# A three-pass f32 matmul kernel on one core: the work of its first tiles in another order

## The chip, the cores and the metric

The kernel runs on one core of a Trainium2 chip. The metric is the device time of one execution in microseconds, as the median of several; lower is better. The engines are TensorE (PE, with its weight loads PEld), VectorE (DVE), ScalarE (ACT), GpSimd (POOL) and SyncE (SP). Each runs its own instructions in the order of the program and waits on semaphores. SP issues most DMAs here, POOL some of them.

## The reference, cut to what matters

Eight images x of 512 tokens by 2048 features go through two adapters of rank 16, chosen per image, and a dense layer.

```
# layer 0: a low-rank update of x, adapters chosen by ids0
Bx  = einsum('bni,bri->bnr', x, B[ids0]);  x = x + einsum('bnr,bor->bno', Bx, A[ids0])
# layer 1: dense layer, bias and a second low-rank update, adapters chosen by ids1
base = einsum('bti,oi->bto', x, W) + b
lora = einsum('bti,bir->btr', x, lora_A[ids1]);  lora = einsum('btr,bro->bto', lora, lora_B[ids1])
out  = x + base + lora * 2
```

## The kernel before, in words

**The big product.** Two images make a group; there are four groups. In a group the product of x1 (x after layer 0) with W plus the identity is computed from halves of W and of x by seven products of sums of halves instead of eight. A product i has 8 output tiles o, so a group has 56 steps and the kernel 224; step s is (g, i, o). A step takes 8 blocks c of 128 input rows. Each operand is split into a high and a low part (w_hi, w_lo, x_hi, x_lo), and a block takes three matmuls of 128x512: L695, L696, L697. Such a step is 24 matmuls.

**Weights.** load_w(s) on SP loads w_one, and w_two where the product needs a sum of two blocks of W; that is so in group 0 for products 0, 1, 2, 4 and 6. make_w(s) on DVE adds the two (L887) and the identity (L891), keep_sum(s) on SP stores the sum in w_sums (L445), and later groups load it from there. Then split_w(s): ACT makes w_hi (L740), DVE w_lo (L896). There are three w_one buffers and two of each other, and load_w(s + 3) is issued in step s, behind keep_sum(s + 1).

**The two adapters' first halves.** "Down": x of an image is multiplied with the adapters of both layers, in 8 chunk pairs d per image. ACT and DVE split each pair (split_chunk(d), L780 and L927), PE runs four matmuls into down_ps (project_down, L640 and L641). Image 1 comes first, as pairs 0 to 7, then image 0. copy_down, add_down and split_rank_x make rank_x from it. "Up": project_up(v) multiplies rank_x with up_w, two matmuls into up_ps (L653), and add_up(v) on DVE adds them to x (L946). v counts the quarters of half an image; B1, A0, B0 and A1 name the four halves of a group, a being the group's first image and b its second. Then sum_x(p, r) and split_x(p, r) (L910, L913; L758, L919) make x_hi and x_lo of product p, quarter r. x_hi and x_lo have six buffers; buffers 4 and 5 lie where a1_raw and a0_raw were.

**The images.** After step 4, 16 matmuls multiply the tables of a0 and a1 (L724), and four more (make_image, L661) fold them into the rank-16 rows that add_rank uses. Their results are copied out by DVE (L1064).

**What sets the order.** It is written by hand: a prologue in each engine's block, and tables by step: ups(s), downs(s), load_at, sum_at and split_at. In a step DVE goes through add(s - 1), split_w(s + 1), split_x, sum_x, add_down, split_down, make_w(s + 2), split_chunk, split_rank_x, split_up, add_up, complete and the copy of an image.

Of the kernel before, what the change touches and what calls it, by code (L numbers as in the profile page):

```python
# [12 lines left out]
NB = 8  # L13
# [40 lines left out]
def load_at(p):  # L54

    return (1, 2, 5, 6) if p % PRODUCTS == 2 else (0, 1, 3, 5)


def sum_at(p):

    if p == 1:
        return (5, 5, 6, 7)
    return {1: (2, 3, 5, 6), 2: (2, 3, 6, 7)}.get(p % PRODUCTS, (1, 3, 5, 6))


def split_at(p):

    if p == 1:
        return (6, 6)
    return {0: (3, 5), 1: (4, 5), 2: (4, 5)}.get(p % PRODUCTS, (2, 4))  # L70
# [37 lines left out]
def ups(s):  # L108

    if s >= STEPS:  # L110
        return []
    if s < 0:
        return [0, 1]
    g, i, o = where(s)
    found = [2, 3] if s == 0 else []
    if i == 0:
        found += [16 * g + 4 * A0 + r for r, at in enumerate((1, 2, 4, 5) if g else (4, 4, 5, 5)) if at == o]
    found += [16 * g + 4 * B0 + r for r, at in enumerate((7, 8, 10, 11)) if at == s % PER_GROUP]
    if i == 2:
        found += [16 * g + 4 * A1 + r for r, at in enumerate((1, 3, 5, 7)) if at == o]  # L120
    if i == 6 and g + 1 < GROUPS:
        found += [16 * (g + 1) + r for r, at in enumerate((2, 4, 5, 6)) if at == o]
    return found
# [134 lines left out]
def build(nc, x, ids0, ids1, a0_down, a0_up, b0, w, bias, a1, b1, identity, mask, w_sums, images, x1, out):  # L258
    with ExitStack() as ctx:
# [99 lines left out]
        down_added = sem("down_added")  # L359
        rank_x_hi_ready = sem("rank_x_hi_ready")  # L360
        rank_x_ready = sem("rank_x_ready")
        rank_loaded = sem("rank_loaded")
# [38 lines left out]
        def down_parts(e):  # L401

            if e < 8:
                return x_hi[e // 2][:, e % 2, :], x_lo[e // 2][:, e % 2, :]
            return bg_hi[e % 3][:, :], bg_lo[e % 3][:, :]

        def rank_x_of(n):
# [12 lines left out]
        def _(sp):  # L420
# [88 lines left out]
            sp.dma_start(ids_sb[:, 1, :], ids1).then_inc(ids_loaded, DMA)  # L509
            for d in (0, 1):  # L510
                load_raw("down", d)
            for d in (2, 3):
                load_early(d)
            sp.wait_ge(ids_loaded, 2 * DMA)
            sp.dma_start(down_raw[0][:, :, :], adapter(0, 1, b0).rearrange("u p c r -> (u p) c r")).then_inc(first_down_loaded, DMA)
            sp.dma_start(down_raw[1][:, :, :], adapter(1, 1, a1).rearrange("u p c r -> (u p) c r")).then_inc(first_down_loaded, DMA)
            for r in range(CH):
                load_resident(0, 1, r)
# [11 lines left out]
            for s in range(STEPS):  # L530
# [8 lines left out]
                if s + W_ONES < STEPS:  # L539
                    load_w(s + W_ONES)  # L540
                if s in (1, 2):
                    for n in range(4 * s - 4, 4 * s):
                        sp.dma_start(a1_raw[:, n, :, :], adapter(1, n, a1).rearrange("u p c r -> (u p) c r"))\
                          .then_inc(a1_loaded, DMA)
# [22 lines left out]
        def _(pool):  # L567
# [38 lines left out]
            load_up(0)  # L606
            load_down(0)
            for n in range(NB):
                pool.dma_start(a0_raw[:, n, :, :], adapter(0, n, a0_down).rearrange("u p c r -> (u p) c r"))\
                    .then_inc(a0_loaded, DMA)  # L610
# [17 lines left out]
        def _(pe):  # L628
            def project_down(d):
                n, k = down_chunk(d)  # L630
                if k == 0:
                    pe.wait_ge(down_ready, turn(n) + 1)
                    if turn(n):
                        pe.wait_ge(down_added, turn(n))
                for u in range(2):
                    pe.wait_ge(bg_ready, 2 * d + u + 1)
                    c = 2 * k + u
                    hi, lo = down_parts(2 * d + u)
                    weights = down[:, c, :, :, :].rearrange("p h l r -> p (h l r)")
                    pe.matmul(down_ps[:, :], weights, hi, start=(c == 0), stop=False)  # L640
                    pe.matmul(down_ps[:, :], weights, lo, start=False, stop=(c == C - 1)).then_inc(bg_used, 1)  # L641

            def project_up(v):
                n, half, r = up_chunk(v)
                if r == 0:
                    pe.wait_ge(up_ready, v // 4 + 1)
                    pe.wait_ge(rank_x_ready, turn(n) + 1)
                for u in range(2):
                    e = 2 * v + u
                    if e >= 2:  # L650
                        pe.wait_ge(up_added, e - 1)
                    o = 2 * r + u
                    pe.matmul(up_ps[e % 2][:, :], up_w[:, P * o:P * (o + 1)], rank_x_of(n)[:, :], start=True, stop=True)\  # L653
                      .then_inc(up_done, 1)

            def make_image(j):
                pe.wait_ge(across_ready, 1)
                pe.wait_ge(b1_rows_loaded, NB * DMA)
                if j:
                    pe.wait_ge(image_ready, j)  # L660
                pe.matmul(image_ps[:, :], across, rows[:, T * j:T * (j + 1)], start=True, stop=True).then_inc(image_done, 1)  # L661

            def add_rank(s):
# [4 lines left out]
                if o == 0:  # L668
                    pe.wait_ge(rank_ready, rank_number(g, i) + 1)
                    pe.wait_ge(rank_x_ready, turn(2 * g + side) + 1)  # L670
                if i == 4:
                    pe.wait_ge(copied, copied_before(s) + 1)
# [58 lines left out]
        def _(act):  # L731
# [42 lines left out]
            def split_chunk(d):  # L774

                wait_for_down_source(act, d)
                for e in (2 * d, 2 * d + 1):
                    if e >= 11:
                        act.wait_ge(bg_used, e - 2)
# [12 lines left out]
            def split_down(n):  # L792
# [4 lines left out]
                if turn(n):  # L797
                    act.wait_ge(down_added, turn(n))
                act.activation(down[:, :, 0, 0, :], down_raw[0][:, :, :], ACT.Copy)
                act.activation(down[:, :, 0, 1, :], down_raw[1][:, :, :], ACT.Copy, scale=SCALE1).then_inc(down_hi_ready, 1)  # L800

            def copy_down(n):
                act.wait_ge(bg_used, 16 * (turn(n) + 1))
                if turn(n):
                    act.wait_ge(rank_x_ready, turn(n))
                act.activation(rank_sum[:, :], down_ps[2 * R:4 * R, :], ACT.Copy).then_inc(down_copied, 1)

            def split_rank_x(n):
# [5 lines left out]
                x_rank = rank_x_of(n)  # L814
                act.activation(x_rank[0:2 * R, :], rank_sum[:, :], ACT.Copy)
                act.activation(x_rank[2 * R:4 * R, :], rank_sum[:, :], ACT.Copy).then_inc(rank_x_hi_ready, 1)

# [11 lines left out]
            split_chunk(3)  # L829
            split_chunk(4)  # L830
            split_up(0)
            split_w(0)
            for d in (5, 6, 7):
                split_chunk(d)
            copy_down(1)
            split_rank_x(1)
            for r in range(CH):
                split_x(0, r)
            split_down(0)
            for d in downs(0):  # L840
                split_chunk(d)
            for s in range(STEPS):
# [6 lines left out]
                if s >= 1 and where(s - 1)[1] == 1:  # L849
                    copy(s - 1)  # L850
                if s == 3:
                    act.wait_ge(a1_loaded, NB * DMA)
                    act.activation(a1_cols.rearrange("p (c n r) -> p c n r", c=C, n=NB),
                                   a1_raw[:, :, :, :].rearrange("p n c r -> p c n r"), ACT.Copy).then_inc(a1_ready, 1)
                if p + 1 < PRODUCTS * GROUPS:
# [9 lines left out]
                if s and s in RANK_X_AT:  # L865
                    split_rank_x(RANK_X_AT[s])
                if s in UP_SPLIT:
                    split_up(UP_SPLIT[s])
# [7 lines left out]
        def _(dve):  # L876
# [131 lines left out]
            split_chunk(2)  # L1008
            split_chunk(3)
            make_w(0)  # L1010
            split_chunk(4)
            split_up(0)
            split_w(0)
            for d in (5, 6, 7):
                split_chunk(d)
            make_w(1)
            add_down(1)
            split_rank_x(1)
            for v in range(CH):
                add_up(v)  # L1020
                split_x(0, v)
            split_down(0)
            for d in downs(0):
                split_chunk(d)
            for s in range(STEPS):
# [4 lines left out]
                if s >= 1:  # L1030
                    add(s - 1)
                if s < STEPS - 1:
                    split_w(s + 1)
                if p + 1 < PRODUCTS * GROUPS:
                    for r in range(2):
# [14 lines left out]
                if s in UP_SPLIT:  # L1050
                    split_up(UP_SPLIT[s])
                if s:
                    for v in ups(s):
                        add_up(v)
                if s >= 1:
# [5 lines left out]
                if 0 <= s - 1 - IMAGE_STEP < 4:  # L1061
                    j = s - 1 - IMAGE_STEP
                    dve.wait_ge(image_done, j + 1)
                    dve.tensor_copy(rows[:, T * j:T * (j + 1)], image_ps[:, :]).then_inc(image_ready, 1)  # L1064
                if (i, o) in RANK_SPLIT:
# [42 lines left out]
```

## Time and profile before

| | us |
|---|---|
| median of 3 runs | 1412.16 (1412.0 to 1413.15) |
| the profiled execution | 1413.14 |
| its span | 1411.1 |
| PE busy | 1368.4 (97%) |
| DVE busy | 951.0 (67%) |
| ACT busy | 552.6 (39%) |
| POOL busy | 86.4 (6%) |
| mean DMA rate | 229 GB/s |

The span runs from the first to the last recorded instruction. Busy times of engines overlap, so they don't add up; an idle engine costs something only where another waits for it. The granted clock of TensorE is 1.00 (2.4 GHz) but for some stretches before 90 us, where it is down to 0.50 (1.2 GHz).

### The profile page before, as it was taken

How to read it: one execution, taken by the hardware profiler on the slowest of the kernel's cores; microseconds unless marked ns; L12 is line 12 of the kernel's file. 1: busy time of each engine (PE TensorE's matmuls, PEld its weight loads, DVE VectorE, ACT ScalarE, POOL GpSimd, SP SyncE). 2: the span in 40 equal slices, each digit the busy share in tenths (PEclk: the TensorE clock that was granted, in tenths of full speed). 3: DMA queues.
4: the chain of work that ended last, by engine and by line, in shares of the span. 5: the costliest groups of instructions: out<-in, count | busy, mean ns of one | idle time of the engine just before them, and what ended most of it. 6: DMA issues, size and time to landing. Idle time of an engine off the chain costs nothing.

```text
span 1411.1 us, 16438 instructions
## 1 busy us (share of the span) xinstructions
PE 1368.4 (97%) x5928; PEld 1116.9 (79%) x5928; DVE 951.0 (67%) x1143; ACT 552.6 (39%) x666; POOL 86.4 (6%) x179
## 2 busy tenths in 40 slices
PE   3888999999999999999999999999999999999999
PEld 2676777888888888888888888888888888888887
DVE  5768876888875666667855676666875566655662
ACT  4443423446334432345523442344633443223321
POOL 2000001000000001010000000110010000000000
PEclk8899999999999999999999999999999999999999
DMA  9768995999973666577853556575973366545542
GB/s 351 217 228 300 356 368 193 324 361 345 329 260 128 220 223 205 182 258 241 290 181 123 183 193 241 167 246 204 326 240 125 124 225 227 192 157 196 197 150 82
DMA packets 101332, 323.15 MB, mean 229 GB/s; under 512 B 13508, under 2 KB 15044, under 8 KB 100996
## 3 DMA queue, kind: packets, MB, share of 16 engines
q1 hardware_dynamic: 95188, 307.68, 62.7%
q0 software_dynamic: 6064, 14.43, 3.6%
q8 instruction: 47, 0.77, 0.2%
q14 instruction: 33, 0.27, 0.1%
HBM read 249.70 MB, written 72.35 MB: 228 GB/s over the span
## 4 chain that ended last, share of the span: by engine, by line
PE 87%; DVE 4%; DMA 4%; ACT 2%; issue 1%; SPq 1%; DVEq 0%; ACTq 0%
PE acc L695 26%; PE acc L696 26%; PE acc L697 26%; DMA w_two<-w 4%; PE acc L675 2%; PE down_ps L640 2%; PE down_ps L641 2%; PE up_ps L653 2%; DVE w_one L887 1%; DVE bg_raw L946 1%; ACT w_hi L740 1%; DVE resident L946 1%; DVE x_lo L919 0%; DMA bg_raw<-x 0%; ACT x_hi L758 0%
## 5 line engine op out<-in xcount | busy, mean ns | idle before, releaser
L695 PE MATMUL acc<-x_hi,w_hi 128*128 128x512 f32 x1792 | 703.0, 392 | 6.6 <-DVE x_lo L919 3.7
L696 PE MATMUL acc<-x_lo,w_hi 128*128 128x512 f32 x1792 | 700.5, 391 | 0.0
L697 PE MATMUL acc<-x_hi,w_lo 128*128 128x512 f32 x1792 | 700.2, 391 | 0.0
L740 ACT ACTIVATE w_hi<-w_one 128x1024 fp32r<-128x1024 f32 x224 | 237.0, 1058 | 544.5 <-PE acc L697 491.1
L896 DVE TENSOR_TENSOR w_lo<-w_one,w_hi 128x1024 fp32r<-128x1024 f32 x224 | 274.2, 1224 | 227.7 <-ACT w_hi L740 227.0
L695 PEld LDWEIGHTS acc<-x_hi,w_hi 128*128 128x128 f32 x1792 | 337.9, 189 | 82.8 <-issue 6.9
L696 PEld LDWEIGHTS acc<-x_lo,w_hi 128*128 128x128 f32 x1792 | 338.0, 189 | 73.1 <-issue 1.0
L697 PEld LDWEIGHTS acc<-x_hi,w_lo 128*128 128x128 f32 x1792 | 337.4, 188 | 71.6
L772 ACT ACTIVATE sums<-acc 128x512 f32<-128x512 f32 x96 | 56.9, 593 | 192.3 <-PE acc L697 186.5
L979 DVE SCALAR_TENSOR_TENSOR sums<-acc,bias_sb,sums 128x512 f32<-128x512 f32 x128 | 95.5, 746 | 25.5 <-PE acc L675 25.1
L919 DVE TENSOR_TENSOR x_lo<-x_stage,x_hi 128x1024 fp32r<-128x1024 f32 x80 | 96.0, 1219 | 2.9 <-ACT x_hi L758 2.7
L758 ACT ACTIVATE x_hi<-x_stage 128x1024 fp32r<-128x1024 f32 x80 | 83.9, 1051 | 13.7 <-PE acc L697 8.1
L913 DVE TENSOR_TENSOR x_stage<-x_stage,resident 128x1024 f32<-128x1024 f32 x64 | 77.9, 1217 | 0.0
L780 ACT ACTIVATE bg_hi<-bg_raw 128x512 fp32r<-128x512 f32 x100 | 58.5, 622 | 38.0 <-DMA bg_raw<-x 34.9
L927 DVE TENSOR_TENSOR bg_lo<-bg_raw,bg_hi 128x512 fp32r<-128x512 f32 x100 | 64.4, 684 | 5.4 <-ACT bg_hi L780 5.4
L589 POOL DMA_DIRECT2D rank_raw<-images x48 | 23.4, 487 | 650.1 <-issue 649.8
L887 DVE TENSOR_TENSOR w_one<-w_one,w_two 128x1024 f32<-128x1024 f32 x40 | 48.8, 1219 | 17.0 <-DMA w_two<-w 17.0
L640 PE MATMUL down_ps<-bg_hi,down 128*128 128x512 f32 x120 | 50.1, 418 | 7.9 <-DVE bg_lo L927 7.9
L603 POOL DMA_DIRECT2D rank_raw<-a_up x48 | 23.5, 491 | 516.5 <-issue 515.9
L966 DVE TENSOR_TENSOR sums<-sums,acc 128x512 f32<-128x512 f32 x32 | 22.0, 686 | 47.7 <-PE acc L697 47.6
L653 PE MATMUL up_ps<-rank_x,up_w 96*128 96x512 f32 x128 | 43.2, 417 | 9.1 <-DVE rank_x L995 3.5
L675 PE MATMUL acc<-rank_x,rank_w 96*128 96x512 f32 x128 | 50.9, 398 | 0.0
(60 smaller groups left out, 668.7 us busy)
## 6 DMA issues: line engine op xcount, KB each, us to landing
w_one<-w_sums SPq DMA_DIRECT2D x120, 512.0 KB, 4.3
w_one<-w SPq DMA_DIRECT2D x104, 512.0 KB, 5.5
bg_raw<-x SPq DMA_DIRECT2D x84, 512.0 KB, 6.1
x_stage<-x SPq DMA_DIRECT2D x68, 512.0 KB, 5.1
out<-sums SPq DMA_DIRECT2D x128, 256.0 KB, 3.6
w_two<-w SPq DMA_DIRECT2D x40, 512.0 KB, 8.1
w_sums<-w_one SPq DMA_DIRECT2D x40, 512.0 KB, 5.6
resident<-x SPq DMA_DIRECT2D x32, 512.0 KB, 8.1
```

What stands on the lines that cost most here:

```text
L640: pe.matmul(down_ps[:, :], weights, hi, start=(c == 0), stop=False)
L653: pe.matmul(up_ps[e % 2][:, :], up_w[:, P * o:P * (o + 1)], rank_x_of(n)[:, :], start=True, stop=True)\
L675: pe.matmul(acc[s % BANKS][:, :], rank_w[:, P * o:P * (o + 1)], rank_x_of(2 * g + side)[:, :], start=False, stop=True, skip_group_check=Tr ...
L695: pe.matmul(ps[:, :], w_hi[ws][:, c, :], hi, start=(c == 0), stop=False)
L696: pe.matmul(ps[:, :], w_hi[ws][:, c, :], lo, start=False, stop=False)
L697: mm = pe.matmul(ps[:, :], w_lo[ws][:, c, :], hi, start=False, stop=(c == H - 1))
L740: act.activation(w_hi[s % W_PARTS][:, :, :], w_one[s % W_ONES][:, :, :], ACT.Copy).then_inc(w_hi_ready, 1)
L758: act.activation(x_hi[q % X_PARTS][:, :, :], x_source(p, r), ACT.Copy).then_inc(x_hi_ready, 1)
L896: dve.tensor_tensor(w_lo[s % W_PARTS][:, :, :], w_one[s % W_ONES][:, :, :], f32(w_hi[s % W_PARTS][:, :, :]), ALU.subtract).then_inc(w_read ...
L913: dve.tensor_tensor(stage, stage, resident[1 if i in (3, 6) else 0][:, cs, :], ALU.subtract if i in (2, 6) else ALU.add).then_inc(x_summed, 1)
L919: dve.tensor_tensor(x_lo[q % X_PARTS][:, :, :], x_source(p, r), f32(x_hi[q % X_PARTS][:, :, :]), ALU.subtract).then_inc(x_ready, 1)
L979: dve.scalar_tensor_tensor(out=tile, in0=acc[s % BANKS][:, :], scalar=bias_sb[:, f:f + 1], in1=tile, op0=ALU.add, op1=ALU.add).then_inc(ba ...
```

## The change

On SP the loads of the first adapters move ahead of the x loads of pairs 1, 2 and 3. In the prologue of ACT and DVE the up weights are split before pair 4, pairs 4 to 7 come before make_w(0) and split_w(0), and split_w(0), split_down(0) and the first pair of image 0 come before the first add_up; add_up(1) comes before split_x(0, 0), and make_w(1) stands behind the last split_x. Pairs 4 and 5 use x_hi and x_lo buffers, and so POOL and SP hold the tables of a0 and a1 until 12 halves of pairs are used. rank_x has a semaphore of its own for ACT's second half. The copy of a1 on ACT comes after split_rank_x in step 3. The up pairs of A0 in group 0 go to steps 4, 5, 6 and 6 (they were in 4, 4, 5 and 5), those of B0 to 8, 9, 11 and 12 in all groups (7, 8, 10 and 11). In each step the first add_up moves ahead of split_w, a second one right behind it. Images alternate between two banks.

```diff
 def load_at(p):
-    return (1, 2, 5, 6) if p % PRODUCTS == 2 else (0, 1, 3, 5)
+    return (2, 3, 5, 6) if p % PRODUCTS == 2 else (0, 1, 3, 5)
...
     if p == 1:
-        return (5, 5, 6, 7)
-    return {1: (2, 3, 5, 6), 2: (2, 3, 6, 7)}.get(p % PRODUCTS, (1, 3, 5, 6))
+        return (4, 5, 6, 7)
+    return {1: (2, 3, 5, 6), 2: (3, 4, 6, 7)}.get(p % PRODUCTS, (1, 3, 5, 6))
...
     if p == 1:
-        return (6, 6)
+        return (5, 6)
...
-        found += [16 * g + 4 * A0 + r for r, at in enumerate((1, 2, 4, 5) if g else (4, 4, 5, 5)) if at == o]
-    found += [16 * g + 4 * B0 + r for r, at in enumerate((7, 8, 10, 11)) if at == s % PER_GROUP]
+        found += [16 * g + 4 * A0 + r for r, at in enumerate((1, 2, 4, 5) if g else (4, 5, 6, 6)) if at == o]
+    found += [16 * g + 4 * B0 + r for r, at in enumerate((8, 9, 11, 12)) if at == s % PER_GROUP]
...
-            if e < 8:
+            if e < 12:
                 return x_hi[e // 2][:, e % 2, :], x_lo[e // 2][:, e % 2, :]
...
+        def image_bank(j):
+            return down_ps if j % 2 else image_ps
...
-            for d in (0, 1):
-                load_raw("down", d)
-            for d in (2, 3):
-                load_early(d)
+            load_raw("down", 0)
             sp.wait_ge(ids_loaded, 2 * DMA)
...
+            load_raw("down", 1)
+            for d in (2, 3):
+                load_early(d)
...
+                if s == 1:
+                    sp.wait_ge(bg_used, 12)
...
+            pool.wait_ge(bg_used, 12)
             for n in range(NB):
...
+                    if turn(n) == 2:
+                        pe.wait_ge(image_ready, 4)
...
                     pe.wait_ge(rank_x_ready, turn(n) + 1)
+                    pe.wait_ge(rank_x_copied, turn(n) + 1)
...
-                if j:
-                    pe.wait_ge(image_ready, j)
+                if j >= 2:
+                    pe.wait_ge(image_ready, j - 1)
...
                 if turn(n):
-                    act.wait_ge(down_added, turn(n))
+                    act.wait_ge(bg_used, 16 * turn(n))
...
-                act.activation(x_rank[0:2 * R, :], rank_sum[:, :], ACT.Copy)
-                act.activation(x_rank[2 * R:4 * R, :], rank_sum[:, :], ACT.Copy).then_inc(rank_x_hi_ready, 1)
+                act.activation(x_rank[0:2 * R, :], rank_sum[:, :], ACT.Copy).then_inc(rank_x_hi_ready, 1)
+                act.activation(x_rank[2 * R:4 * R, :], rank_sum[:, :], ACT.Copy).then_inc(rank_x_copied, 1)
```

The prologue on DVE; ACT's has the same order. First before, from the split of pairs 2 and 3 (x_lo from x_stage) to the first add_up (L946):

```order
L927 TENSOR_TENSOR x_lo<-x_stage,x_hi 128x512 x4
L887 TENSOR_TENSOR w_one<-w_one,w_two 128x1024
L891 SCALAR_TENSOR_TENSOR w_one<-identity_sb,w_one 128x128
L927 TENSOR_TENSOR bg_lo<-resident,bg_hi 128x512 x2
L932 TENSOR_TENSOR up_w<-rank_raw,up_w 16x1024
L896 TENSOR_TENSOR w_lo<-w_one,w_hi 128x1024
L927 TENSOR_TENSOR bg_lo<-resident,bg_hi 128x512 x6
...
L991 TENSOR_TENSOR rank_sum<-down_ps,rank_sum 32x512
L995 TENSOR_TENSOR rank_x<-rank_sum,rank_x 32x512
L946 TENSOR_TENSOR resident<-resident,up_ps 128x512 x2
L919 TENSOR_TENSOR x_lo<-resident,x_hi 128x1024
```

And the same place of the changed kernel, whose line numbers are 12 higher here:

```order
L939 TENSOR_TENSOR x_lo<-x_stage,x_hi 128x512 x4
L944 TENSOR_TENSOR up_w<-rank_raw,up_w 16x1024
L939 TENSOR_TENSOR x_lo<-resident,x_hi 128x512 x4
L939 TENSOR_TENSOR bg_lo<-resident,bg_hi 128x512 x4
L899 TENSOR_TENSOR w_one<-w_one,w_two 128x1024
...
L1003 TENSOR_TENSOR rank_sum<-down_ps,rank_sum 32x512
L1007 TENSOR_TENSOR rank_x<-rank_sum,rank_x 32x512
L908 TENSOR_TENSOR w_lo<-w_one,w_hi 128x1024
...
L939 TENSOR_TENSOR bg_lo<-resident,bg_hi 128x512 x2
L958 TENSOR_TENSOR resident<-resident,up_ps 128x512 x4
L931 TENSOR_TENSOR x_lo<-resident,x_hi 128x1024
```

The sum of the weights (make_w(0)) moved behind all pairs of image 1, w_lo(0) behind rank_x, and split_down(0) with a pair of image 0 moved from behind the last x_lo to ahead of the first add_up; two add_up now stand in a row.

DVE in steps 4 and 5, before:

```order
L946 TENSOR_TENSOR resident<-resident,up_ps 128x512 x4
L896 TENSOR_TENSOR w_lo<-w_one,w_hi 128x1024
L910 TENSOR_TENSOR x_stage<-resident 128x1024 x2
L887 TENSOR_TENSOR w_one<-w_one,w_two 128x1024
L891 SCALAR_TENSOR_TENSOR w_one<-identity_sb,w_one 128x128
L946 TENSOR_TENSOR resident<-resident,up_ps 128x512 x4
L1060 TENSOR_TENSOR sums<-down_ps,sums 128x128
```

And in steps 4 to 6 of the changed kernel:

```order
L958 TENSOR_TENSOR resident<-resident,up_ps 128x512 x2
L908 TENSOR_TENSOR w_lo<-w_one,w_hi 128x1024
L922 TENSOR_TENSOR x_stage<-resident 128x1024
L899 TENSOR_TENSOR w_one<-w_one,w_two 128x1024
L903 SCALAR_TENSOR_TENSOR w_one<-identity_sb,w_one 128x128
L958 TENSOR_TENSOR resident<-resident,up_ps 128x512 x2
L908 TENSOR_TENSOR w_lo<-w_one,w_hi 128x1024
...
L1079 TENSOR_TENSOR sums<-down_ps,sums 128x128
L958 TENSOR_TENSOR resident<-resident,up_ps 128x512 x2
L908 TENSOR_TENSOR w_lo<-w_one,w_hi 128x1024
L958 TENSOR_TENSOR resident<-resident,up_ps 128x512 x2
```

The four adds in a row came apart, and each first one stands ahead of the w_lo of its step.

## Rows read from the trace of the kernel before

**Rows 1.** The page, busy us by engine, share and instructions.
```profile
PE 1368.4 (97%) x5928; PEld 1116.9 (79%) x5928; DVE 951.0 (67%) x1143; ACT 552.6 (39%) x666; POOL 86.4 (6%) x179
```

**Rows 2.** Waits of PE, whole run: us in total, times, longest us.
```profile
PE image_ps L661 <- DVE sums L1064: 2.6, 2, 1.6
PE acc L695 <- DVE w_lo L896: 2.4, 2, 1.3
...
PE up_ps L653 <- DVE up_w L932: 1.3, 1, 1.3
```

**Rows 3.** Timeline of PE: start us, us, engine, line, operation [idle before <-releaser].
```profile
13.22 0.79 PE L640 MATMUL down_ps<-x_hi,down 128*128 128x512 f32 x1 [13.22 <-DVE down L985]
...
35.09 1.14 PE L653 MATMUL up_ps<-rank_x,up_w 96*128 96x512 f32 x2 [3.50 <-DVE rank_x L995]
...
39.69 0.77 PE L695 MATMUL acc<-x_hi,w_hi 128*128 128x512 f32 x1 [1.65 <-DVE x_lo L919]
...
42.39 1.06 PE L653 MATMUL up_ps<-rank_x,up_w 96*128 96x512 f32 x2
...
56.66 0.39 PE L695 MATMUL acc<-x_hi,w_hi 128*128 128x512 f32 x1
...
79.06 0.39 PE L695 MATMUL acc<-x_hi,w_hi 128*128 128x512 f32 x1
...
82.01 0.70 PE L653 MATMUL up_ps<-rank_x,up_w 96*128 96x512 f32 x2 [1.43 <-issue]
...
85.98 1.39 PE L653 MATMUL up_ps<-rank_x,up_w 96*128 96x512 f32 x2 [1.89 <-DVE resident L946]
...
91.12 3.73 PE L724 MATMUL down_ps<-a_raw,sums 128*128 128x128 f32 x32
94.61 0.48 PE L695 MATMUL acc<-x_hi,w_hi 128*128 128x512 f32 x1
...
117.07 1.10 PE L661 MATMUL image_ps<-sums 128*128 128x512 f32 x2 [1.58 <-DVE sums L1064]
...
211.59 0.47 PE L695 MATMUL acc<-x_hi,w_hi 128*128 128x512 f32 x1 [1.30 <-DVE w_lo L896]
```

**Rows 4.** Timeline of DVE, and its waits for w_two after 150 us.
```profile
20.03 1.22 DVE L887 TENSOR_TENSOR w_one<-w_one,w_two 128x1024 f32<-128x1024 f32 x1 [4.45 <-DMA w_two<-w]
...
25.20 1.89 DVE L927 TENSOR_TENSOR bg_lo<-resident,bg_hi 128x512 fp32r<-128x512 f32 x3
...
DVE w_one L887 <- DMA w_two<-w: 12.6, 12, 1.7
```

**Rows 5.** Timeline of ACT.
```profile
11.65 0.42 ACT L799 ACTIVATE down<-down_raw 128x256 fp32r<-128x256 f32 x1 [3.94 <-DMA down_raw<-a]
...
15.40 2.10 ACT L789 ACTIVATE up_w<-rank_raw 16x1024 fp32r<-16x1024 f32 x2
...
76.50 1.91 ACT L853 ACTIVATE sums<-a_raw 128x2048 f32<-128x2048 f32 x1
```

**Rows 6.** DMA issues of SP; 128 KB loads to landing; the bg_raw tile before 60 us.
```profile
5.49 0.35 SPq L516 DMA_DIRECT2D down_raw<-a  x1
...
31.75 0.33 SPq L445 DMA_DIRECT2D w_sums<-w_one  x1
...
110.06 0.33 SPq L445 DMA_DIRECT2D w_sums<-w_one  x1
...
a_raw<-a SPq DMA_DIRECT2D x8, 128.0 KB, 3.2
...
DMA to landing us min/median/max: 3.7/11.4/18.9
```

**Rows 7.** Busy us by engine in a stretch, then PEclk, DMA share, GB/s.
```profile
105.00:110.00 5.00, 5.00 (x21) 3.45 (x19) 4.97 (x6) 4.46 (x5) 0.00 (x0) 1.00 0.01 5
110.00:115.00 5.00, 3.70 (x17) 3.05 (x17) 4.90 (x6) 3.08 (x3) 1.46 (x3) 1.00 0.80 223
...
190.00:200.00 10.00, 8.92 (x40) 7.09 (x39) 7.85 (x9) 2.01 (x2) 0.00 (x0) 1.00 1.00 382
```

More of the change, by code:

```diff
@@ L360, in build @@
         rank_x_hi_ready = sem("rank_x_hi_ready")
+        rank_x_copied = sem("rank_x_copied")
         rank_x_ready = sem("rank_x_ready")
@@ L658, in make_image @@
                 pe.wait_ge(b1_rows_loaded, NB * DMA)
-                if j:
-                    pe.wait_ge(image_ready, j)
-                pe.matmul(image_ps[:, :], across, rows[:, T * j:T * (j + 1)], start=True, stop=True).then_inc(image_done, 1)
+                if j >= 2:
+                    pe.wait_ge(image_ready, j - 1)
+                pe.matmul(image_bank(j)[:, :], across, rows[:, T * j:T * (j + 1)], start=True, stop=True).then_inc(image_done, 1)
             def add_rank(s):
@@ L670, in add_rank @@
                     pe.wait_ge(rank_x_ready, turn(2 * g + side) + 1)
+                    pe.wait_ge(rank_x_copied, turn(2 * g + side) + 1)
                 if i == 4:
@@ L777, in split_chunk @@
                 for e in (2 * d, 2 * d + 1):
-                    if e >= 11:
+                    if e >= 15:
                         act.wait_ge(bg_used, e - 2)
@@ L805, in copy_down @@
                     act.wait_ge(rank_x_ready, turn(n))
+                    act.wait_ge(rank_x_copied, turn(n))
                 act.activation(rank_sum[:, :], down_ps[2 * R:4 * R, :], ACT.Copy).then_inc(down_copied, 1)
@@ L829, in _ @@
             split_chunk(3)
-            split_chunk(4)
             split_up(0)
-            split_w(0)
-            for d in (5, 6, 7):
+            for d in (4, 5, 6, 7):
                 split_chunk(d)
@@ L836, in _ @@
             split_rank_x(1)
+            split_w(0)
+            split_down(0)
+            first, second = downs(0)
+            split_chunk(first)
             for r in range(CH):
                 split_x(0, r)
-            split_down(0)
-            for d in downs(0):
-                split_chunk(d)
+            split_chunk(second)
             for s in range(STEPS):
@@ L850, in _ @@
                     copy(s - 1)
[L851 to L854, printed above, removed]
                 if p + 1 < PRODUCTS * GROUPS:
@@ L866, in _ @@
                     split_rank_x(RANK_X_AT[s])
+                if s == 3:
+                    act.wait_ge(a1_loaded, NB * DMA)
+                    act.activation(a1_cols.rearrange("p (c n r) -> p c n r", c=C, n=NB),
+                                   a1_raw[:, :, :, :].rearrange("p n c r -> p c n r"), ACT.Copy).then_inc(a1_ready, 1)
                 if s in UP_SPLIT:
@@ L1009, in _ @@
             split_chunk(3)
+            split_up(0)
+            for d in (4, 5, 6, 7):
+                split_chunk(d)
             make_w(0)
[L1011 to L1016, printed above, removed]
             add_down(1)
             split_rank_x(1)
-            for v in range(CH):
-                add_up(v)
-                split_x(0, v)
+            split_w(0)
             split_down(0)
-            for d in downs(0):
-                split_chunk(d)
+            first, second = downs(0)
+            split_chunk(first)
+            add_up(0)
+            add_up(1)
+            split_x(0, 0)
+            add_up(2)
+            split_x(0, 1)
+            add_up(3)
+            split_x(0, 2)
+            split_x(0, 3)
+            make_w(1)
+            split_chunk(second)
             for s in range(STEPS):
@@ L1031, in _ @@
                     add(s - 1)
+                us = ups(s) if s else []
+                for v in us[:1]:
+                    add_up(v)
                 if s < STEPS - 1:
                     split_w(s + 1)
+                for v in us[1:]:
+                    add_up(v)
                 if p + 1 < PRODUCTS * GROUPS:
@@ L1051, in _ @@
                     split_up(UP_SPLIT[s])
-                if s:
-                    for v in ups(s):
-                        add_up(v)
                 if s >= 1:
@@ L1063, in _ @@
                     dve.wait_ge(image_done, j + 1)
-                    dve.tensor_copy(rows[:, T * j:T * (j + 1)], image_ps[:, :]).then_inc(image_ready, 1)
+                    dve.tensor_copy(rows[:, T * j:T * (j + 1)], image_bank(j)[:, :]).then_inc(image_ready, 1)
                 if (i, o) in RANK_SPLIT:
```

## The prediction, made before the changed kernel ran

> **What bounds the kernel now.** The totals first [rows 1]: TensorE (PE) is busy 1368.4 of 1411.1 us. Only the other 42.7 us, and matmuls run at half clock, can be won. The list of PE's waits [rows 2] and the timeline [rows 3] put all of them before some 220 us; after the wait at 211.59 one of half a us is left. So the question is how much earlier PE gets past step 23. What follows moves with it.
>
> Four stretches matter. PE starts at 13.22, because ScalarE (ACT) waits until 11.65 for the adapters [rows 3, 5]. The down projection of image 1 (8 chunk pairs, d 0 to 7, four matmuls each) is fed in pieces: after half of it VectorE (DVE) sits 4.45 us waiting for the weights w_two, in front of work that PE wants [rows 4], and the first up projection starts at 35.09. Step 1 starts at 56.66. Steps 4 to 8 have holes: 1.43 and 1.89 us in step 4, 1.3 in step 7 for up_w, 2.6 for two images [rows 2, 3]. Then the DMA engines are full (share 1.00, 382 GB/s, still at 190 to 200 [rows 7]) and DVE waits 12 times for w_two, 12.6 us in all, after 150 us [rows 4]; 2.4 us of that reach PE as waits for w_lo [rows 2].
>
> **Part 1: the adapters ahead of three x loads on SP.** They need the ids and are issued at 4.36 and 5.49 in either order; before, 2 MB of x stood ahead, now 0.5 MB. They were there at 11.65 [rows 5, 6]. Bounds: no gain, or landing at 8.7 (5.49 + 3.2, the median of the later 128 KB loads on that queue [rows 6]). I take 9, and nothing hangs on it: chunk pair 1 is now issued at 5.9, and as the fastest 512 KB load took 3.7 us [rows 6] and the adapters share the way, it lands near 9.9. ACT: 1.1 for pair 1, 0.7 for the adapters; DVE 0.8 behind it; PE starts at 12.7, **0.5 us earlier**. The x of pairs 4 to 7 follows at 1.3 us each (512 KB at 390 GB/s) until 17.4; ACT wants the first at 17.1, the last at 20.3.
>
> **Part 2: pairs 4 to 7 before the weight work.** ACT: pairs 2 and 3 until 14.0, up_w 3.17 (two in 2.10, and a third [rows 5]) until 17.1, then 8 halves at 0.54 until 21.4. DVE: up_w 1.2 until 18.4, then 8 halves at 0.61 (three take 1.89 [rows 4]) until 23.3. PE ends the last near 24.1; before it was 31.4. Then ACT copies 0.6, DVE adds 0.7 (behind make_w(0), 1.5 us, of which the copy hides all but the last), rank_x takes 1.3 + 0.7 + gaps, and the first up projection starts at 27.4: **7.7 us earlier** [rows 3].
>
> **Part 3: step 0, where most of that is paid back.** Ahead of the first add_up DVE now has split_w(0) 1.2 with 1 us of waiting for w_hi(0), split_down(0) 0.7 and a chunk pair 1.2: add_up(0) starts at 31.4. With add_up(1) it is 34.2, with x_lo(0,0) 35.4. The new wait: add_up(2) needs a projection that PE issues only after the first six matmuls of step 0, and these need x_lo(0,0). Six took 2.7 us at half clock (39.69 to 42.39 [rows 3]), which I keep, as PE has just stood idle. So 2.7 + 0.8 until DVE sees the projection + 1.3 + 1.2 go round before x_lo(0,1) is out at 41.3; the same round brings add_up(3) to 44.7; x_lo(0,2) and (0,3) end at 47.2 and 48.4, make_w(1) and pair 9 at 51.1. PE: chunks 4, 5 from 47.3 to 49.9, four down matmuls to 51.6, chunk 6, pair 9 and chunk 7 to 53.9. Step 1 starts **2.8 us earlier**. Steps 1 to 3 took 22.4 us (56.66 to 79.06) and keep them: step 4 at 76.2.
>
> **Part 4: steps 4 to 8.** In step 4 the copy of a1 (1.91) leaves its place before rank_sum on ACT [rows 5]; rank_x(0) is then ready at 77.2 and PE wants it at 77.6. One up pair stands in step 4 instead of two, so the second's wait and the half clock behind it go. From step 4's start to step 5's it was 15.55 us [rows 3]; now 5.44 for the 24 matmuls, 0.45 for the pair, 3.5 for the a0/a1 product (91.12 to 94.61) = 9.4, and step 5 starts at 85.6 against 94.61, **9.0 us earlier**. In step 6 two up pairs stand with DVE's add between them, a new wait of 0.8; the 1.3 for up_w goes (it is ready a step ahead), and the 2.6 for the images go (two banks). The second image, at 117.07 before, comes at 104.4, and step 9 some 13.5 us earlier than before by PE's own order.
>
> **Part 5: what is late next: the weights.** The store of w_sums(8) and all loads behind it are queued on SP behind make_w(8), at 110.06 before [rows 6]. In the new order it is made at 101.9 (DVE in step 6 from 94.3: two add_up 2.6, w_lo 1.2, x_lo 1.2, sum 1.2, make_w 1.5), so SP gets there 8.0 us earlier and not 13.5. The bytes behind it are those of before and one bg_raw load (1.4 us). Before, the engines had a share of 0.80 from 110 to 115 [rows 7] and up to 0.05 free in some later stretches: about 2 us that can be caught up. 8.0 - 1.4 + 2.0 = **8.6 us** for the last weights of group 0, and PE, there too early, waits some 5 us for them in steps 12 to 23. In groups 1 to 3 PE never waits, and the moves on DVE (add_up ahead of split_w) are covered: w_lo is out about 4.6 us into a step of 5.9. They count nothing.
>
> The added waits: POOL and SP hold the rows of a0 and a1 until 12 halves are used (about 20 us). The eight a0 loads at 1.15 each are out by 30, wanted at 82. SP's keep_sum(1) stands behind make_w(1): it was at 31.75 [rows 6] and is now near 50. The load of w(3) behind it leaves at 50.7 and lands 6 to 7 us later; DVE wants it at 58.8. The cover is 1 to 2 us. The Trainium skill ("DMA: Bandwidth & Descriptors", on the SWDGE path) says that DMA engines do not wait on semaphores, the issuing sequencer does. The trace agrees, as SP's rows after 31.75 show no load until 38.31; this speaks against the change, since every later load stands behind that store.
>
> The same page (Specifications) gives about 358 GB/s per core as HBM's limit; by it the extra load would cost 0.1 us more. The row at 190 us has 382, so the measurement decides.
>
> **Against the measured time.** The span of 1411.1 belongs to an execution of 1413.14; the median is 1412.16. After: span 1411.1 - 8.6 = 1402.5, on the scale of the median **1403.6**.
>
> **Rivals.**
> A (forecast, 0.48): the weight stretch lets 8.6 of 13.5 through: 1401 to 1406.
> B (0.18): it doesn't bind; its loads were late only because make_w was. For it: the engines stand still from 105 to 110 (share 0.01 [rows 7]), so there was room before. Against: 12 waits for w_two with the engines full. 13.5 us stay, and up to 2.4 of w_lo waits go: 1396 to 1399.
> C (0.21): the start gives less. If PE is at half clock through pairs 4 to 7 (16 x 0.2 = 3.2 us), or w(3) comes 3 us after DVE wants it, step 1 starts no earlier than before, and some 5.5 are left: 1405.5 to 1409.
> D (0.07): within 0.2% (2.8 us, about what a measurement of this kernel can tell from no change): the start is lost and the weight stretch takes most of the rest: 1410 to 1414.
> E (0.06): slower, by add_up ahead of split_w on DVE. In the steps of group 0 with an up pair (4, 5, 6, 8, 9, 11, 12, 17, 19, 21, 23) DVE stands until PE's projection, 2.1 us into the step, adds for 1.3 and only then splits the weights; make_w comes 2.1 us later. It decides when w_lo is over 1.3 us later than I have it. Then each of 11 steps costs up to 1.3, 14 us, more than the 8.6: 1418.
>
> **Numbers.** Median 1403.6. The range takes in B and C: 1396.5 to 1409. Faster by over 0.2%: A, B, C, 0.87; within: D, 0.07; slower: E, 0.06.
>
> **What would show it.** First matmul near 12.7, first up projection near 27.4, step 1 near 54, step 5 near 85.6, the second image near 104 with no wait for a copy. SP's store of w_sums(8) near 102. DVE's waits for w_two begin near 120 and sum to more than 12.6, and PE's for w_lo to more than 2.4: if not, B. If the up projection is early but step 1 not before 56, Part 3 was too kind. If PE waits for w_lo in steps with an up pair, and w_two had landed, E.

## The result, and the profile after

The changed kernel takes **1422.6 us** (median; 1421.75 to 1423.62). The kernel before took 1412.08 in the same comparison. The ratio is 1.0073, with a 95% interval of 1.0056 to 1.0091: slower by 10 us, where 1403.6 was forecast. The profiled execution has a span of 1419.9, against 1411.1 before.

Where the time goes is seen from the start of the run on. First the timeline of PE of the changed kernel (start us, us, engine, line, operation, and in brackets the idle time before with its releaser), which answers to [rows 3]:

```profile
12.60 0.79 PE L649 MATMUL down_ps<-x_hi,down 128*128 128x512 f32 x1 [12.60 <-DVE down L997]
...
27.01 0.71 PE L663 MATMUL up_ps<-rank_x,up_w 96*128 96x512 f32 x2 [2.82 <-DVE rank_x L1007]
...
41.09 0.79 PE L706 MATMUL acc<-x_hi,w_hi 128*128 128x512 f32 x1 [2.15 <-DVE x_lo L931]
...
76.27 0.39 PE L706 MATMUL acc<-x_hi,w_hi 128*128 128x512 f32 x1
...
86.06 0.48 PE L706 MATMUL acc<-x_hi,w_hi 128*128 128x512 f32 x1
...
104.39 1.02 PE L671 MATMUL down_ps<-sums 128*128 128x512 f32 x2
...
114.75 0.47 PE L706 MATMUL acc<-x_hi,w_hi 128*128 128x512 f32 x1 [1.78 <-DVE w_lo L908]
...
137.34 0.77 PE L706 MATMUL acc<-x_hi,w_hi 128*128 128x512 f32 x1 [4.08 <-DVE w_lo L908]
```

Up to the second image at 104.39 it goes as forecast; there PE is 12.7 us ahead of before (117.07 in [rows 3]). All of that and 9 us more (1419.9 - 1411.1) is lost between 110 and 230 us. The waits of DVE and of PE in 100 to 230 us of the changed kernel (waiting engine and what for, us in total, times, longest) answer to [rows 2, 4]:

```profile
DVE bg_raw L958 <- DMA bg_raw<-x: 29.6, 7, 6.7
DVE w_one L899 <- DMA w_two<-w: 3.1, 2, 1.8
...
PE acc L706 <- DVE w_lo L908: 17.9, 6, 4.8
PE acc L706 <- DVE x_lo L931: 2.3, 1, 2.3
PE acc L706 <- ACT sums L783: 1.1, 1, 1.1
```

DVE now waits seven times for the load of bg_raw, 29.6 us. The kernel before had one such wait, of 0.9 us, and waited 9.6 us for w_two in the same stretch, where it is 3.1 now. The timeline of DVE of the changed kernel shows what stands behind it:

```profile
127.35 0.69 DVE L973 TENSOR_TENSOR sums<-sums,acc 128x512 f32<-128x512 f32 x1 [0.87 <-PE acc L708]
134.78 1.28 DVE L958 TENSOR_TENSOR bg_raw<-bg_raw,up_ps 128x512 f32<-128x512 f32 x2 [6.74 <-DMA bg_raw<-x]
135.98 1.22 DVE L908 TENSOR_TENSOR w_lo<-w_one,w_hi 128x1024 fp32r<-128x1024 f32 x1
137.12 1.22 DVE L925 TENSOR_TENSOR x_stage<-x_stage,resident 128x1024 f32<-128x1024 f32 x1
138.25 1.22 DVE L899 TENSOR_TENSOR w_one<-w_one,w_two 128x1024 f32<-128x1024 f32 x1
```

add_up (L958) now comes right behind the add of the step before (L973), and w_lo (L908), which PE wants, and make_w (L899) stand behind it. And here is SP's queue in the same place: the load issued at 124.49 is the one that DVE has from 134.78 on.

```profile
124.49 0.49 SPq L482 DMA_DIRECT2D bg_raw<-x  x1
...
128.86 0.72 SPq L482 DMA_DIRECT2D bg_raw<-x  x1
139.82 0.33 SPq L449 DMA_DIRECT2D w_sums<-w_one  x1
140.19 0.43 SPq L494 DMA_DIRECT2D x<-bg_raw  x1
140.72 0.83 SPq L438 DMA_DIRECT2D w_one<-w  x1
```

DVE was free from 128.04 (134.78 - 6.74), 3.6 us after the issue; the load took 10.3 us. And it closes into a loop: the stall of DVE holds make_w, SP waits for make_w to store the sum (no row between 128.86 and 139.82), so the next weights and the next bg_raw load leave late, and the next add_up waits again. The DMA engines are still full while DVE waits: their share is 1.01 from 130 to 140 us and 1.00 from 176 to 180, in the wait that ends at 180.38. Right behind it they are half idle, 0.54 from 180 to 184 and 0.46 from 184 to 188, until SP's next loads are out. The clock of PE falls after its longer waits. The busy time by stretch of the changed kernel (PE, PEld, DVE, ACT, POOL, then PEclk, DMA share and GB/s):

```profile
180.00:190.00 10.00, 7.05 (x21) 5.61 (x22) 9.06 (x10) 2.00 (x2) 0.00 (x0) 0.66 0.61 223
190.00:200.00 10.00, 7.94 (x35) 6.26 (x34) 4.49 (x8) 1.06 (x1) 0.00 (x0) 1.00 0.94 336
200.00:210.00 10.00, 10.00 (x46) 8.23 (x45) 6.47 (x9) 3.07 (x3) 0.00 (x0) 1.00 0.74 237
210.00:220.00 10.00, 5.93 (x20) 4.43 (x19) 7.23 (x9) 1.06 (x1) 0.00 (x0) 0.83 0.66 267
```

The chain that ended last gives 34.3% of 100 to 230 us to the load of bg_raw (5.1% before).

### The profile page after: what moved, and what is told of

The parts are those of the page before. It is cut to its first block, busy times and chain, and to the rows that moved or that the text cites. A ratio compares the mean times of both kernels' runs of the same rounds, so it can differ in the third digit from the quotient of the medians.

```text
span 1419.9 us, 16464 instructions
## 1 busy us (share of the span) xinstructions
PE 1368.7 (96%) x5928; PEld 1117.7 (79%) x5928; DVE 949.8 (67%) x1143; ACT 552.7 (39%) x666; POOL 86.8 (6%) x179
## 4 chain that ended last, share of the span: by engine, by line
PE 89%; DMA 4%; DVE 4%; SPq 1%; issue 1%; ACT 1%; DVEq 0%; ACTq 0%
PE acc L706 27%; PE acc L707 27%; PE acc L708 27%; DMA bg_raw<-x 3%; PE acc L686 2%; PE down_ps L649 2%; PE up_ps L663 2%; PE down_ps L650 2%; DVE w_one L899 1%; DMA w_two<-w 1%; DVE w_lo L908 1%; DVE resident L958 0%; DVE x_lo L931 0%; SPq L443 0%; SPq L438 0%
## 5 line engine op out<-in xcount | busy, mean ns | idle before, releaser
L706 PE MATMUL acc<-x_hi,w_hi 128*128 128x512 f32 x1792 | 705.1, 393 | 27.7 <-DVE w_lo L908 17.9
L908 DVE TENSOR_TENSOR w_lo<-w_one,w_hi 128x1024 fp32r<-128x1024 f32 x224 | 273.8, 1223 | 142.7 <-ACT w_hi L751 142.2
L958 DVE TENSOR_TENSOR resident<-resident,up_ps 128x512 f32<-128x512 f32 x64 | 41.1, 683 | 73.8 <-PE up_ps L663 73.8
L958 DVE TENSOR_TENSOR bg_raw<-bg_raw,up_ps 128x512 f32<-128x512 f32 x64 | 41.1, 683 | 55.8 <-DMA bg_raw<-x 29.6
L899 DVE TENSOR_TENSOR w_one<-w_one,w_two 128x1024 f32<-128x1024 f32 x40 | 48.7, 1218 | 6.9 <-DMA w_two<-w 6.7
```

The source lines that it names most:

```text
L706: pe.matmul(ps[:, :], w_hi[ws][:, c, :], hi, start=(c == 0), stop=False)
L908: dve.tensor_tensor(w_lo[s % W_PARTS][:, :, :], w_one[s % W_ONES][:, :, :], f32(w_hi[s % W_PARTS][:, :, :]), ALU.subtract).then_inc(w_read ...
L958: dve.tensor_tensor(chunk[:, u, :], chunk[:, u, :], up_ps[u][:, :], ALU.add).then_inc(up_added, 1)
```

## The experiments

**Theory:** the loss is the wait of add_up at the head of the step for a load that SP issues one step earlier. **Rivals:** the place at the head costs by itself (the prediction's rival E, over the wait for PE's projection); the new prologue or the new steps of the quarters cost the time; full DMA engines take the early gain back in any order.

### 1. The add_up of the bg_raw quarters back to its old place

```diff
-                us = ups(s) if s else []
+                us = [v for v in ups(s) if up_resident(v)] if s else []
...
                 split_up(s + 2)
+                if s:
+                    for v in ups(s):
+                        if not up_resident(v):
+                            add_up(v)
```

> The changed kernel, but the add_up of the quarters that come through bg_raw (B0 and A1, 32 in all) stands again behind make_w and split_up in its step on DVE; those on resident tiles (A0, B1) stay ahead of split_w. Theory 1 (in the changed kernel DVE waits 29.6 us for loads of bg_raw at the head of seven steps, and split_w and make_w stand behind that wait): these waits go to under 3 us, PE's 20.2 us of waits for w_lo and x_lo between 110 and 223 us fall to some 5, and the time is 1403.6 if the stretch of full DMA engines lets 8.6 us of the early gain through, 1398.5 if it lets all through. Theory 2 (the loss comes from the new steps of the B0 quarters, 8, 9, 11, 12, or from the x_stage loads that moved with them): the time stays above 1415. Theory 3 (the early gain is lost to full DMA engines in any order): 1410 to 1414.

Measured: **1404.32** (1403.5 to 1404.6), ratio to the kernel before 0.9935 [0.9917, 0.9952]. Waits in 100 to 230 us of this kernel:

```profile
DVE w_one L899 <- DMA w_two<-w: 11.4, 9, 2.7
...
DVE bg_raw L958 <- DMA bg_raw<-x: 2.6, 3, 1.5
...
PE acc L706 <- DVE w_lo L908: 3.0, 4, 0.9
```

The kernel before took 1413.54 here. One edit of places takes 18.3 us off by the medians, 19.5 by the two ratios (1.0073 - 0.9935, of 1412). The spans differ by 17.7 (1419.9 and 1402.2). Of that 13.7 is idle time of PE, above all its waits for w_lo (17.9 to 3.0), and 4.0 is its busy time (1368.7 to 1364.7). The latter goes with the clock, which stays at 1.00 here in all of 100 to 230 us and was 0.84, 0.66 and 0.83 in three stretches of 10 us of the changed kernel. What remains of the change in this kernel is worth, within the interval (7 to 12 us), what the prediction said of the whole.

### 2. The load earlier, the add left at the head

```diff
-                for v in ups(s + 1):
+                for v in ups(s + 2):
                     if not up_resident(v):
                         load_raw("up", v)
```

> The changed kernel with add_up where it has it, but SP issues the bg_raw load of an up quarter two steps ahead of its step, not one. Theory 1 (what costs is that the load is not there): DVE's waits for bg_raw fall from 29.6 to under 10 us and the time to 1402 to 1409. Rival (what costs is add_up itself ahead of split_w, because it waits for PE's projection in the step, as the prediction's case E had it): the time stays within 3 us of 1422.6. If the buffers of bg_raw are the limit, SP waits for the store of x1 instead, and the time is between, 1410 to 1418.

Measured: **1402.87** (1401.97 to 1403.69), ratio 0.9924 [0.9907, 0.9942]. DVE waits nowhere for the load of bg_raw in this kernel, and PE's waits for w_lo are 4.4 us. With the add still at the head, this parts the two reasons: it is the load that costs, not the place.

### 3. The kernel before with only this add moved

```diff
+                for v in ups(s) if s else []:
+                    if not up_resident(v):
+                        add_up(v)
...
-                        add_up(v)
+                        if up_resident(v):
+                            add_up(v)
```

> The kernel before with one thing of the change: the add_up of the quarters in bg_raw moved ahead of split_w in its step. Theory 1: the waits for bg_raw appear here too, 20 to 30 us on DVE, 10 to 18 us of them on PE, so 1422 to 1430. Rival (the wait needs the earlier start, since only then PE runs ahead of the loads): under 1415.

Measured: **1428.87** (1426.82 to 1429.67), ratio 1.0105 [1.0086, 1.0123]: 15 us slower than before (1413.54), with nothing else of the change in it. The timeline of DVE of this kernel:

```profile
186.51 1.29 DVE L946 TENSOR_TENSOR bg_raw<-bg_raw,up_ps 128x512 f32<-128x512 f32 x2 [6.52 <-DMA bg_raw<-x]
...
202.65 1.28 DVE L946 TENSOR_TENSOR bg_raw<-bg_raw,up_ps 128x512 f32<-128x512 f32 x2 [5.59 <-DMA bg_raw<-x]
...
218.74 1.28 DVE L946 TENSOR_TENSOR bg_raw<-bg_raw,up_ps 128x512 f32<-128x512 f32 x2 [5.49 <-DMA bg_raw<-x]
```

In the whole run there are seven such waits, 25.1 us, and PE waits 11.6 us for w_lo. The cause adds its loss in either kernel, 15 us here and 18 to 20 there, so neither the new prologue nor the new steps are needed for it.

### 4. Each quarter of x_lo behind its own add

From the kernel of experiment 1; both edits show against the change.

```diff
-            add_up(0)
-            add_up(1)
-            split_x(0, 0)
-            add_up(2)
-            split_x(0, 1)
-            add_up(3)
-            split_x(0, 2)
-            split_x(0, 3)
+            for v in range(CH):
+                add_up(v)
+                split_x(0, v)
```

> As the run with the add_up behind make_w, and in addition x_lo(0,0) again ahead of add_up(1) in the prologue of DVE (the order add_up, split_x, add_up, split_x). Theory from the prediction's third part: DVE's two waits of 3.5 us for PE's projection in step 0 go, step 1 starts near 49 and not at 53.3. If the weights' loads limit what comes after, the time is that of the run beside it within 1.5 us; if PE's own order does, it is 4 us lower.

Measured: **1400.25** (1399.61 to 1402.38), ratio 0.9912 [0.9893, 0.9931], 4 us under experiment 1. The round of Part 3 (x_lo(0,0) waits for add_up(1), and the third add for PE's six matmuls) is cut here, by going back to the order of the kernel before; the second image comes at 101.28 instead of 104.80. What is won that early still arrives at the end. It doesn't tell whether PE's own order or the weights set that end: SP's store of w_sums(8) is earlier by as much, at 98.57 instead of 102.08, so the weights move with it.

### 5. All three edits

Experiments 1, 2 and 4 together.

> The change with three edits together: the add_up of the quarters that come through bg_raw stands behind make_w again, SP issues their loads two steps ahead, and in the prologue each x_lo quarter follows its own add_up. If the wait at the head of the step is the whole loss, the first two edits answer the same thing and don't add: 1400.25 (x_lo each with the add_up behind) less the 1 us of DVE's wait for bg_raw that can reach PE, 1399 to 1401. If the full DMA queues set the end (rival), an earlier bg_raw load only pushes a w_two load back: the same 1400 to 1402, and DVE's waits for w_two grow from 10.4 us by what its waits for bg_raw lose.

Measured: **1399.31** (1398.66 to 1399.66), ratio 0.9900 [0.9883, 0.9916]. The range overlaps that of experiment 4 only at its very end, but 1 us is within what these runs leave open. DVE's waits for w_two are 12.8 us: as the rival said, they grow as the waits for bg_raw go.

### 6. The new prologue alone

The kernel before with the new order of SP's first loads and of the prologue on ACT and DVE; the tables by step, the places of add_up in a step and the single image bank stay. The core of the difference to the change:

```diff
-            split_chunk(4)
-            split_w(0)
-            for d in (5, 6, 7):
+            for d in (4, 5, 6, 7):
...
+            split_w(0)
```

> The kernel before with the new order of the prologue and of SP's first loads alone; the tables by step, the places of add_up in a step and the one bank for images are those of before. By the prediction's Parts 1 to 3, step 1 starts 2.8 to 3.3 us earlier than before (near 53.5) and nothing else moves: the time is 2 to 3.5 us under the kernel before, ratio 0.9975 to 0.9985. Rival: the weights behind SP's late keep_sum(1) or the DMA engines later take it back, ratio 0.999 to 1.001. No wait of DVE for the load of bg_raw over 2 us in either case.

Measured: **1411.58** (1408.09 to 1413.87), ratio 0.9987 [0.9977, 0.9997]: 1.8 us faster, and one wait for bg_raw, of 1.0 us. The interval takes in both what was expected and the rival, so it is open whether part of the early gain is lost later here; that this prologue doesn't make the loss of the change is clear. Step 1 starts in this kernel at

```profile
54.31 0.40 PE L706 MATMUL acc<-x_hi,w_hi 128*128 128x512 f32 x1
```

2.35 us earlier than before (56.66 in [rows 3]); in the changed kernel it is 53.31. So of the 12.7 us that the change has won at the second image, the larger part is in steps 4 to 8, as Part 4 had it.

### 7. The load of bg_raw ahead of the weights in SP's step

```diff
+                for v in ups(s + 1):
+                    if not up_resident(v):
+                        load_raw("up", v)
                 if s + W_ONES < STEPS:
                     load_w(s + W_ONES)
...
-                for v in ups(s + 1):
-                    if not up_resident(v):
-                        load_raw("up", v)
```

> The change with one edit on SP: in a step the load of bg_raw is issued ahead of the two weight loads instead of behind them. Theory (the load lands late because of what stands ahead of it in the queue): two loads of 512 KB less ahead of it, 2.7 us at 390 GB/s for both, so each of 7 waits of 6.7 us shrinks by about 2.7 us, and the time falls by up to 19 us, down to where the weights bind: 1404 to 1412. Rival (it lands late because SP issues it late, behind its wait for keep_sum): the waits stay over 5 us each and the time is within 3 us of 1422.6.

Measured: **1405.06** (1401.79 to 1407.31), ratio 0.9934 [0.9915, 0.9954]. The timeline of DVE of this kernel, in the place of the 6.74 above and at a later one:

```profile
130.15 1.29 DVE L958 TENSOR_TENSOR bg_raw<-bg_raw,up_ps 128x512 f32<-128x512 f32 x2 [3.17 <-DMA bg_raw<-x]
...
198.04 1.28 DVE L958 TENSOR_TENSOR bg_raw<-bg_raw,up_ps 128x512 f32<-128x512 f32 x2 [1.59 <-DMA bg_raw<-x]
```

Six waits of 13.0 us in all are left, and PE's for w_lo are 4.3. The four long ones (6.7, 6.5, 4.7 and 5.1 us in the changed kernel) are shorter by 3.0 to 4.6 us, more than the 2.7 of two weight loads that was expected: a shorter wait also lets SP issue the next loads sooner. What is left is mostly absorbed by the rest of the step, and the time is that of experiment 1 within the intervals.

### 8. Half the bytes of w_two

From the kernel of experiment 1. Half of the second weight block is not loaded from the tenth sum on, so those sums lack it.

```diff
-                    sp.dma_start(w_two[k % W_TWOS][:, :, :], w[H * two[1] + o][:, H * two[0]:H * (two[0] + 1), :])\
+                    h = H // 2 if k >= 9 else H
+                    sp.dma_start(w_two[k % W_TWOS][:, 0:h, :], w[H * two[1] + o][:, H * two[0]:H * two[0] + h, :])\
```

> The kernel that measured 1404.32 (add_up of the bg_raw quarters behind make_w) with half of each w_two load left out from the tenth on, so that the sums of weights are wrong there: 256 KB less in each of those steps of group 0. If full DMA engines keep back 4 to 5 us of what the start won (13.5 us at the second image, 8.9 at the end), DVE's waits for w_two fall from 11.4 to under 4 us and the time to 1399 to 1401. Rival (the rest was lost to waits between the engines, not to bytes): 1403.5 to 1405.

Measured: **1397.68** (1395.02 to 1398.76), ratio 0.9884 [0.9866, 0.9902], 6.6 us under experiment 1. Waits of this kernel from 100 to 230 us:

```profile
DVE w_one L900 <- DMA w_two<-w: 5.5, 6, 1.7
...
PE acc L707 <- DVE w_lo L909: 0.2, 1, 0.2
```

So bytes of weights do cost time here, as Part 5 said. The size fits less well: the time is below the 1399 to 1401 that were expected, DVE's waits for w_two fell only to 5.5 us, and 16 us under the kernel before is more than the 13.5 of the early gain. The missing bytes also take away waits that the kernel before has, so this run doesn't measure what share of the early gain the bytes keep back.

### 9. The add at the head, loads two steps ahead, x_lo each

Experiments 2 and 4 without 1.

> The change with SP's bg_raw loads two steps ahead and each x_lo quarter behind its own add_up in the prologue; the add_up stays at the head of the step, as in the change. Theory (the place at the head costs nothing once the load is there): 1398 to 1401, as the kernel with all three edits (1399.31). Rival (the place at the head costs something by itself, since w_lo and make_w come later by the add of 1.3 us and the wait for the projection): 1403 to 1406, with waits of DVE for up_ps of some 2 us a step and more waits of PE for w_lo.

Measured: **1398.91** (1398.19 to 1401.24), ratio 0.9901 [0.9884, 0.9917]: no different from experiment 5, which has the add behind make_w. The place at the head costs nothing that can be measured once the load is there. By rival E it would have had to.

### 10. The add behind, the load of bg_raw first

The kernel of experiment 4 with the edit of experiment 7.

> The kernel that measured 1400.25 (add_up of the bg_raw quarters behind make_w, each x_lo quarter behind its own add_up) with SP's bg_raw load ahead of the two weight loads of its step. The add_up behind make_w doesn't need it earlier, and w_one and w_two land 1.3 us later each time; if the full DMA queues set the end, this only changes the order of the same bytes: 1399.5 to 1402.5, DVE's waits for w_two 10.4 us or up to 3 us more. Rival (the loads of weights are what DVE waits for, so putting anything ahead of them costs): 1404 to 1408.

Measured: **1402.51** (1401.17 to 1403.38), ratio 0.9924 [0.9908, 0.9941]; DVE's waits for w_two 17.0 us against 10.4, more than the 3 us on top that were expected. Where the add doesn't need the load early, putting it first only delays the weights: some 2 us, on the edge of what can be told and between what was expected and the rival.

Of the kernels that load all the weights, those of experiments 5 and 9 are the fastest, 14 us under the kernel before and 23 to 24 under the change.

## Why the prediction was wrong

**What bounds it, Parts 1 to 4: right.** First matmul 12.60 (12.7 was forecast), first up projection 27.01 (27.4), step 1 at 53.31 (53.9), step 4 at 76.27 (76.2), step 5 at 86.06 (85.6), second image at 104.39 (104.4). The new round in step 0 shows as the idle times before 41.09 and its like. The two banks took the waits for the image away.

**Part 5, the weights: right for another kernel.** SP's store of w_sums(8) came at 101.67 (102 was forecast). The kernel of experiment 1, the change but for one add, gained 9.2 us (1413.54 - 1404.32, of one comparison) where 8.6 was forecast. In its trace the w_lo of step 12 starts 13.7 us earlier than before (126.9 and 140.6) and that of step 23 8.6 us earlier (201.6 and 210.2), so the stretch of the weights lets through what Part 5 said. Its terms (8.0, 1.4 and 2.0 us) were not measured one by one, and PE waited 3.0 us for w_lo where some 5 was forecast; that the sum came out so near is in part luck. Experiment 8 shows that bytes of weights cost time there.

**The step that failed** is in Part 5: "the moves on DVE (add_up ahead of split_w) are covered ... They count nothing". It was drawn for groups 1 to 3, where it holds, and left out group 0 from step 8 on, where the quarters come through bg_raw. There add_up has two inputs, PE's projection and a load. Only the first was priced; rival E, which does take up these steps, prices the projection too and not the load. The load is issued one step earlier, behind a store and two weight loads. In the old place w_lo, work on x and make_w stood ahead of the add, and so did DVE's wait for w_two, whose load was issued before that of bg_raw. The timeline of DVE before shows it for step 19:

```profile
189.91 1.23 DVE L896 TENSOR_TENSOR w_lo<-w_one,w_hi 128x1024 fp32r<-128x1024 f32 x1 [0.53 <-ACT w_hi L740]
191.05 1.22 DVE L913 TENSOR_TENSOR x_stage<-x_stage,resident 128x1024 f32<-128x1024 f32 x1
194.00 1.23 DVE L887 TENSOR_TENSOR w_one<-w_one,w_two 128x1024 f32<-128x1024 f32 x1 [1.73 <-DMA w_two<-w]
195.26 0.29 DVE L891 SCALAR_TENSOR_TENSOR w_one<-identity_sb,w_one 128x128 f32<-128x128 f32 x1
195.47 1.28 DVE L946 TENSOR_TENSOR bg_raw<-bg_raw,up_ps 128x512 f32<-128x512 f32 x2
```

From 189.38 (189.91 - 0.53) to the add at 195.47 are 6.1 us, 1.73 of them the wait for w_two: time in which the load of bg_raw could land unnoticed. Call it the cover. SP had issued that w_two at 184.72 and bg_raw right behind it, at 185.64: when DVE had waited for the one, the other still had the 1.5 us of make_w to land. The prediction named no price for that cover gone. The rows had signs: DMA engines at a share of 1.00 [rows 7], and bg_raw loads of 3.7 to 18.9 us to landing in the crowded start, before 60 us [rows 6]. In the profile before, from 100 to 230 us, the eight bg_raw loads took 2.9 to 9.7 us, median 6.6, and DVE waited just 0.9. A wait that is nearly nothing says that the cover was nearly long enough everywhere, but not that any of it can be spared. Taking some 6 us of it away was priced at 0.

It is a missing term, not a mis-sized one: 18.3 us by the medians and 19.5 by the ratios of the change and of experiment 1, and 15 in the kernel before (experiment 3). It turned a gain of 9.2 us into the loss of 10.5 that was measured (1422.6 against 1412.08).

**The rivals.** E had the sign, near enough the time (1418) and the engine, but its cause falls, and that its time was near is luck: it had DVE wait for PE's projection in group 0, and in the changed kernel that wait isn't among those from 100 to 230 us. Its 24 waits (26.2 us) are in groups 1 to 3, where PE waits for nothing after 230 us. Experiments 2 and 9 show the place at the head harmless. B (all of 13.5 stays, 1396 to 1399) isn't what experiment 1 measured once the new wait was gone (1404.32), and experiment 8 speaks against its premise that the weights don't bind. C and D didn't come to be.

**The sign that was named for E.** "If PE waits for w_lo in steps with an up pair, and w_two had landed, E." The first half came true; the thing that had not landed was bg_raw, which no line of the prediction asked about. The sign for B misled too: DVE's waits for w_two sum to 6.7 us in the changed kernel, under the 12.6 of before, but because DVE stood for bg_raw instead. In experiment 1 they are 13.8 us and PE's for w_lo 3.0, both just over the values named (12.6 and 2.4).

## What to carry to other kernels

When an instruction is moved ahead on an in-order engine, list everything it waits for, and for each input take the time from its issue to the new place against the time it takes to land under the load of that stretch, not only against the engine that feeds it. A wait of nearly zero in the profile before is no proof of slack: the cover may be just long enough. And where the waiting engine also lets the next loads go (here make_w releases SP), the wait feeds itself: 3.0 to 4.6 us less in each of four long waits won nearly the whole loss back (experiment 7). Issuing the load one step earlier, or ahead of the others in the queue, is then the cheap cure.

## What the runs showed that was not expected

The stall left the DMA engines partly idle just where they had been the limit. The share is 0.61 from 180 to 190 us of the changed kernel, where experiment 1 has 1.02; later the difference is smaller (0.74 and 0.78 from 200 to 210, 0.66 and 0.76 from 210 to 220). From 100 to 230 us they moved 302 GB/s on average, against 326 before. They are idle behind the long waits, not in them: in the one that ends at 180.38 SP had issued its last load at 175.21, and the next left at 186.33, behind make_w and the store of the sum.

And the granted clock of PE fell to 0.84, 0.66 and 0.83 in the three stretches of 10 us in which it had waited 4.08 us (at 137.34), 4.75 (at 182.95) and 4.07 (at 214.78). Waits of 2.28 (at 169.02) and 2.06 us (at 199.08) in the same kernel, and of up to 2 us in experiment 1, left it at 1.00.
